# Attention sums divided untransposed, eight heads at a time, and the rows of maxima loaded from ScalarE's queue

## What is computed

```python
def _L0_xattn_ref(x, cross_input, ...):        # H, D = 16, 16
    q, k, v = _heads(x @ Wq + bq), _heads(x @ Wk + bk), _heads(x @ Wv + bv)
    att = einsum('bhqd,bhkd->bhqk', q, k) * scale, causal mask
    y = einsum('bhqk,bhkd->bhqd', softmax(att), v)
    qc, kc, vc = ...                            # the same against cross_input, 1601 keys, no mask
    y = y + einsum('bhqk,bhkd->bhqd', softmax(attc), vc)
    return y.transpose(0, 2, 1, 3).reshape(B, T, C) @ Wp + bp

x = x + tanh(g_xattn[0]) * _L0_xattn_ref(_layernorm(x), ctx_512, ...)
x = x + tanh(g_ffn[0]) * _L0_ffn_ref(_layernorm(x), ...)   # shared expert + 2 of 7 routed experts, 704 wide
```

## Time and profile before

| | |
|---|---|
| median of three runs | 1414.64 us (1413.62 to 1415.73) |
| the profiled execution | 1413.27 us |
| its span, first to last instruction | 1411.5 us |
| PE busy | 1368.6 us (97%) |
| DVE, ACT, POOL busy | 880.9, 727.3, 365.4 us |
| granted TensorE clock, mean | 0.993 |

### The profile page before, as it was taken

How to read it: one execution, slowest core, us unless ns; L and a number is a source line. 1 busy time by engine, 2 the same in 40 slices (tenths; PEclk the granted TensorE clock), 3 DMA queues, 4 the chain that set the end, 5 groups by cost and what they waited for, 6 DMA issues and landing times.

```text
span 1411.5 us, 27301 instructions
## 1 busy us (share of the span) xinstructions
PE 1368.6 (97%) x7688; PEld 694.0 (49%) x7689; DVE 880.9 (62%) x1804; ACT 727.3 (52%) x1107; POOL 365.4 (26%) x743
## 2 busy tenths in 40 slices
PE   7988999999999999999999999989999999999997
PEld 4544333333333333333333333364556777777775
DVE  6776888888888888888888888653532222222221
ACT  4644667677777676767676767732210222222221
POOL 5655222222222222222222222200001232233232
PEclk9999999999999999999999999999999999999999
DMA  8754111111111111111111111057004122112111
GB/s 246 237 186 154 43 53 51 48 50 48 47 49 50 51 50 50 49 48 48 48 51 51 50 49 50 7 218 297 0 1 134 26 33 34 30 30 37 30 30 23
DMA packets 57711, 98.43 MB, mean 70 GB/s; under 512 B 7441, under 2 KB 42001, under 8 KB 56657
## 3 DMA queue, kind: packets, MB, share of 16 engines
q1 hardware_dynamic: 50384, 88.10, 18.8%
q0 software_dynamic: 7296, 9.97, 4.5%
HBM read 69.20 MB, written 28.58 MB: 69 GB/s over the span
## 4 chain that ended last, share of the span: by engine, by line
PE 88%; DMA 2%; DVE 2%; ACT 1%; issue 1%; POOL 1%; SPq 0%; POOLq 0%; ACTq 0%; DVEq 0%
PE ps L669 19%; PE ps L834 13%; PE ps L651 13%; PE ps L551 13%; PE ps L847 7%; PE ps L786 5%; PE ps L797 3%; PE ps L718 3%; PE ps L654 2%; PE ps L565 2%; PE ps L858 2%; DMA k_parts<-work 2%; PE ps L555 1%; PE ps L592 1%; PE ps L625 1%
## 5 line engine op out<-in xcount | busy, mean ns | idle before, releaser
L1242 DVE TENSOR_REDUCE mx<-ps 128x1 f32<-128x512 f32 (+1 forms) x832 | 515.1, 662 | 99.6 <-PE ps L551 69.3
L993 ACT ACTIVATE arena<-ps 128x1024 f32<-128x1024 f32 (+1 forms) x512 | 484.3, 995 | 138.7 <-PE ps L651 135.2
L669 PE MATMUL ps<-arena 128*32 128x512 f32 (+5 forms) x2432 | 290.9, 525 | 0.6 <-ACT arena L993 0.4
L551 PE MATMUL ps<-arena 96*128 96x512 bf16 x768 | 263.0, 382 | 7.3 <-DMA arena<-k_parts 2.9
L651 PE MATMUL ps<-arena 98*128 98x512 bf16 x832 | 264.4, 381 | 5.0 <-DMA arena<-rowst 4.9
L1144 POOL TENSOR_SCALAR_AFFINE_SELECT arena<-arena 128x128 f32<-128x128 f32 x256 | 74.8, 292 | 439.2 <-ACT arena L993 429.3
L834 PE MATMUL ps<-arena,work 128*128 x608 | 186.4, 460 | 0.6 <-issue 0.6
L551 PEld LDWEIGHTS ps<-arena 96*128 96x128 bf16 x768 | 74.1, 96 | 178.0 <-DVE mx L1242 103.2
L1520 DVE TENSOR_TENSOR work<-work,ps 128x352 f32<-128x352 f32 x76 | 39.6, 521 | 179.1 <-ACT work L1061 179.1
L834 PEld LDWEIGHTS ps<-arena,work 128*128 128x128 f32 x608 | 112.5, 190 | 57.4 <-issue 1.1
L1242 DVE TENSOR_REDUCE mneg<-ps 128x2 f32<-128x512 f32 (+2 forms) x192 | 112.4, 640 | 23.9 <-PE ps L561 23.4
(11 more groups left out here) (161 smaller groups left out, 1406.8 us busy)
## 6 DMA issues: line engine op xcount, KB each, us to landing
arena<-in_experts SPq DMA_DIRECT2D x8, 2176.0 KB, 12.2
arena<-k_parts SPq DMA_DIRECT2D x64, 198.1 KB
arena<-k_parts SPq DMA_DIRECT2D x64, 132.1 KB
arena<-q_parts SPq DMA_DIRECT2D x64, 96.0 KB
k_parts<-work SPq DMA_DIRECT2D x16, 300.0 KB, 5.2
q_parts<-work SPq DMA_DIRECT2D x12, 384.0 KB, 5.4
arena<-k_parts SPq DMA_DIRECT2D x64, 66.0 KB
arena<-q_parts SPq DMA_DIRECT2D x64, 64.0 KB
```

The source lines that it names most:

```text
L551: mm = pe.matmul(out, qx[:, qt * P:(qt + 1) * P], ks[0:KROWS, T + j * CHUNK:T + (j + 1) * CHUNK], start=True, stop=True)
L669: mm = pe.matmul(ps[32 * q:32 * q + VW, 6, b0:b1], vst[0:kn, r % VR, TT + kt if cross else kt, :], pr[0:kn, c0:c0 + b1 - b0], start=(phase ...
L993: act.activation(pr[:, c0:c0 + n], ps[:, 2 * (g % 2):2 * (g % 2) + 2, :].rearrange("p b n -> p (b n)")[:, 0:n], ACT.Exp, scale=SCALE).then ...
L1242: return dve.tensor_reduce(m, out, AX_X, ALU.max)
```

## The change

- The `norm` step is gone from PE, and with it `norm_out`, POOL's operations per head and the reciprocal per head. Its place among the banks stays, as `spare`. Whoever would have waited for `norm` now waits for the entry six places before.
- `osb` of each head is stored to DRAM (`o_parts`, 256 KB) by SP. ACT's next copy into `osb` waits for the store.
- Eight heads are a group. Their denominators come back as 128 x 32 for each of four parts, their numerators as 128 x 512 (16 rows a head), the first part straight into `yT`, the channel-by-token layout that `project` reads. POOL adds the cross parts, DVE takes one reciprocal of 128 x 64, SP stores it and loads it back spread over each head's 16 rows. POOL multiplies twice and adds once.
- The steps are now 4 alone, seven turns of eight heads, 4 alone. The group's loads are issued in the turn's fourth head, the sums are made in its sixth, the reciprocal in its seventh, the products in its eighth.
- `rows` on ACT issues the load of `rowst` itself, behind its own copy.
- The fourth stack slot lies in `shared`. The shared expert's weights are loaded behind the store of head 60.
- At the end there is no turning of y. Sequences 0 to 2 are projected, then `turn_xn(0)` and one piece of `shared_up(0)`, then sequence 3. The last head's parts of the last group are copied out of `osb` by SP (denominators) and ACT (numerators). ACT also issues the first store of `xn_rows`.

```diff
@@ schedule
-            out += [("values", 0), ("norm",)]
+            out += [("values", 0), ("spare",)]
@@
+SUMS_IN, RECIP_IN, OUT_IN, RECIP_AT = 5, 6, 7, 3
 def run_steps(eng, step):
-    step(0, 0, False, True, True)
-    step(1, 1, True, True, True)
-    heads = NR
-    turns = (NU - 2 - 2) // heads
...
+    for u in range(BEGUN):
+        step(u, u % NR, u > 0, True, True)
+    with eng.Fori(0, TURNS) as i:
+        for h in range(GH):
+            step(i * GH + (BEGUN + h), h % NR, True, True, True, i, h)
+    for u in range(GH * TURNS + BEGUN, NU):
+        step(u, u % NR, True, u + 1 < NU, u + 2 < NU)
@@ sync
-            rows_load(0, 0)
...
+            def sums_store(v):
+                sp.wait_ge(S["o_evac"], v + 1)
+                sp.dma_start(o_parts[bass.ds(v, 1)].rearrange("a p t -> (a p) t"), osb).then_inc(S["o_written"], 16)
+            def parts_load(j, n=GH):
+                sp.wait_ge(S["parts_free"], j + 1)
+                sp.wait_ge(S["o_written"], j * (16 * GH) + 16 * n)
+                heads = o_parts[bass.ds(j * GH, n)]
+                for q in range(4):
+                    src = heads[:, VW * q + D:VW * q + D + 1, :].rearrange("u a (d t) -> (u a) d t", t=DW)
+                    sp.dma_start(den[0:n * D, q, :], src).then_inc(S["den_in"], 16)
+                for q, dst in enumerate([yT[:, bass.ds(j, 1), :].rearrange("p a t -> p (a t)"), *cross_num, self_num]):
+                    sp.dma_start(dst[0:n * D, :], heads[:, VW * q:VW * q + D, :]).then_inc(S["num_in"], 16)
+            def recip_store(j):
+                sp.wait_ge(S["recip_done"], j + 1)
+                for s in range(2):
+                    sp.dma_start(recip_rows[...], recip[:, s, :]).then_inc(S["recip_out"], 16)
+            def recip_load(j):
+                sp.wait_ge(S["recip_out"], j * 32 + 32)
+                for s, dst in enumerate((cross_recip, self_recip)):
+                    sp.dma_start(dst, src.to_broadcast([GH, D, T])).then_inc(S["recip_in"], 16)
...
+                    stack_loads(i * GH + (BEGUN + NR + h), h % NR)
+                    sums_store(i * GH + (BEGUN + h))
+                    if BEGUN + h == GH - 1:
+                        parts_load(i)
+                    if h + 1 == RECIP_IN:
+                        recip_store(i)
+                        recip_load(i)
+            for u in range(TURNS * GH + BEGUN, NU - 1):
+                sums_store(u)
+                if u == TURNS * GH + BEGUN:
+                    sp.dma_start(weights[:, SHARED, :], a["experts"][SHARED]).then_inc(S["shared_load"], 16)
+            parts_load(NGRP - 1, GH - 1)
@@ tensor
-                    elif item[0] == "norm" and prev:
-                        bank_free(u, "norm")
-                        norm(u)
...
-            for b in range(B):
-                if b == B - 1:
-                    turn_xn(0)
+            for b in range(B - 1):
                 project(b)
+            turn_xn(0)
             pe.wait_ge(S["shared_load"], 16)
-            shared_up(0)
+            shared_up(0, 0, SPLIT_UP)
+            project(B - 1)
+            shared_up(0, SPLIT_UP, IT)
@@ scalar
                 act.activation(rowst[:, :], out[0:MROWS * 2 * TT, 0:P], ACT.Copy).then_inc(S["rows_evac"], 1)
+                act.wait_ge(S["rows_evac"], v + 1)
+                act.dma_start(qst[r][KROWS:KROWS + MROWS, :, :].rearrange("p i t -> p (i t)"), rowst[:, :]
+                              ).then_inc(S["rows_ready"], 16)
...
+                if not (isinstance(u, int) and u == 1):
+                    act.wait_ge(S["o_written"], u * 16 - 16)
                 act.activation(osb[:, :], ps[:, 6, :], ACT.Copy).then_inc(S["o_evac"], 1)
@@ gpsimd
+                pool.tensor_tensor(den[:, 0, :], den[:, 0, :], den[:, 1, :], ALU.add).then_inc(S["den_half"], 1)
+                pool.tensor_tensor(den[:, 2, :], den[:, 0, :], den[:, 2, :], ALU.add).then_inc(S["den_sum"], 1)
...
+                pool.tensor_tensor(y, y, cross_num[0], ALU.add).then_inc(S["num_half"], 1)
+                pool.tensor_tensor(y, y, cross_num[1], ALU.add).then_inc(S["num_sum"], 1)
...
+                pool.tensor_tensor(y, y, cross_recip, ALU.mult).then_inc(S["y_cross"], 1)
+                pool.tensor_tensor(self_num, self_num, self_recip, ALU.mult).then_inc(S["y_self"], 1)
+                pool.tensor_tensor(y, y, self_num, ALU.add).then_inc(S["y_done"], 1)
@@ vector
+            def reciprocals(j):
+                dve.wait_ge(S["den_sum"], j + 1)
+                dve.reciprocal(recip[:, :, :], den[:, 2:4, :]).then_inc(S["recip_done"], 1)
...
+            for t in range(early):
+                residual(t)
...
+                if t == 4:
+                    reciprocals(NGRP - 1)
+            tail_stats(early - 1)
+            for t in range(early - SCALE_LAG, early):
+                tail_scale(t)
+            shared_hidden(0, 0, SPLIT_UP)
+            for t in range(early, NT):
+                residual(t)
```

More of the change, by code:

```diff
@@ L117 @@
 PE_ORDER = schedule()
-ENTRIES = [item for item in PE_ORDER if item[0] in ("max", "norm", "rows")]
+ENTRIES = [item for item in PE_ORDER if item[0] in ("max", "spare", "rows")]
 RING = 3
@@ L124 @@
 SCALE_LAG = 5
-RSUM_AT = HALF + 4
-def run_steps(eng, step):
-    step(0, 0, False, True, True)
-    step(1, 1, True, True, True)
-    heads = NR
-    turns = (NU - 2 - 2) // heads
[L134 to L137, removed]
+SPLIT_UP = 1
+GH = P // D
+NGRP = NU // GH
+BEGUN = GH // 2
+TURNS = NGRP - 1
+SUMS_IN, RECIP_IN, OUT_IN, RECIP_AT = 5, 6, 7, 3
+assert GH % NR == 0 and BEGUN % NR == 0 and BEGUN >= 2
+def run_steps(eng, step):
+    for u in range(BEGUN):
[4 more added lines that the diff above has]
+    for u in range(GH * TURNS + BEGUN, NU):
         step(u, u % NR, True, u + 1 < NU, u + 2 < NU)
@@ L577, in bank_free @@
                         pe.wait_ge(S["max_red"], min(n, NU * NMAX - MAXED) if isinstance(n, int) else n)
-                elif before[0] == "norm" and not (isinstance(u, int) and u == 0):
-                    pe.wait_ge(S["norm_evac"], step)
                 elif before[0] == "rows":
@@ L709, in step @@
                     pe.wait_ge(S["pool_chain"], 3 * NR + 3)
-            def norm(u):
-                if isinstance(u, int) and u > 1:
-                    pe.wait_ge(S["norm_evac"], u - 1)
-                pe.wait_ge(S["o_evac"], u)
-                out = bank_of("norm")
-                for t in range(TT):
-                    mm = pe.transpose(out[:, t * P:(t + 1) * P], osb[:, t * P:(t + 1) * P], ident[:, :])
-                mm.then_inc(S["norm_mm"], 1)
             pe.wait_ge(S["prep_freed"], len(pieces))
@@ L973, in sums_out, with step @@
                 act.wait_ge(S["pv_done"], u * NPH)
+                if not (isinstance(u, int) and u == 1):
+                    act.wait_ge(S["o_written"], u * 16 - 16)
                 act.activation(osb[:, :], ps[:, 6, :], ACT.Copy).then_inc(S["o_evac"], 1)
[L976 to L984 removed]
+            def step(u, r, prev, nxt, nxt2, group=None, h=None):
                 for g in range(NG):
@@ L1155, in step @@
                 mask(u, 1, 2)
-                if prev:
-                    cross_sums(u)
                 mask(u, 2, TT)
-                if prev:
-                    head_output(u)
-                    pool.wait_ge(S["y_done"], u)
+                if h == SUMS_IN:
+                    den_sums(group)
+                    num_sums(group)
+                if h == OUT_IN:
+                    outputs(group)
             pool.wait_ge(S["prep_freed"], len(pieces))
@@ L1378, in tail_scale, with residual @@
                 scale_rows(t)
-            for t in range(NT):
+            def residual(t):
                 dve.wait_ge(S["proj_mm"], t + 1)
```

202 lines of the change are left out of this document (105 added, 97 removed).

## The result

The changed kernel takes 1471.45 us (median of four runs, 1465.92 to 1474.85) where the kernel before took 1414.13 in the same comparison: 1.040 times as long, 95% interval 1.0364 to 1.0435. The forecast was 1386.1 us, with a range of 1374 to 1404.

A forecast was written before the change was run, and what follows sets the result against it. PE looked like the only bound, but after the norm the loop hangs on DVE. Gains of 4.5 (start), 17.5 (loop), 1.0 (last heads) and 5.5 (tail), 28.5 in all, gave 1384.8 profiled, 1386.1 us as median; range 1374 to 1404.

The forecast's parts named there:

- the loop's side work: Loop: added ACT issue, POOL operations, DVE reciprocal and SP transfers (8.4 us of issue once in eight heads) cost nothing.
- 1.8 to 3.4: Loop, SP: expected landing time in us of a transfer, from two earlier loads, on an idle queue and behind stores.
- 3.2 was the limit: Loop, score matmul: the rows' load delays PE only if it lands later than 3.2 us after issue.
- Rival 4: Score matmul in every head: rows land late, each of 61 heads loses 0.6 us, 1423 us; chance 0.06.
- rival 3: Loop: POOL's 128x512 operations reach masks or small DVE operations, 21 us lost, 1407; sign: longer heads, one kind in eight; 0.07.
- The gain in the loop: Steps 1 to 61: without the norm DVE's reductions start earlier, 0.287 us a head, 17.5 us in all.
- the last heads: Steps 62 and 63: no pair pieces there, so the norm's 0.50 us goes whole, 1.0 us in all.
- rival 1: Loop: PE alone counts, 0.50 us gained in each of 61 steps, 30.5 us, time 1373; chance 0.14.
- rival 2: Loop: the stall moves and the loop gains nothing; start, last heads and tail remain, 1403.6 us; chance 0.16.
- The start: Before the loop: rows from ACT's queue land earlier, first exp at 136.0; 4.5 us gained (3 to 7).
- The tail: After the last values: norm chain and y turns go, third shared product 5.5 us sooner (2 to 9.2).
- the delay costs nothing: Tail, SP queue: expert loads start some 12 us later, harmless because 70 us without a load follow.

The follow-up runs named there:

- run 3: Changed kernel with every stack load cut into 16-row ones, twelve issues a head instead of six: 1395.31 us, 0.9883 times the kernel before.
- run 8: Changed kernel with only the keys' stack loads cut into 16-row ones: 1410.59 us, 0.9999 times the kernel before.
- run 9: Changed kernel with only the queries' stack loads cut into 16-row ones: 1437.65 us, 1.0174 times the kernel before.
- Run 1: Changed kernel with the load of the maxima's rows issued by SP again, behind the stack loads and the sums' store: 1511.19 us.
- run 6: Changed kernel with all stack loads cut into 16-row ones and expert loads issued only after the first store of normalised rows landed: 1382.45 us, 0.978.
- run 7: Changed kernel with the group's eight loads and the reciprocals' store and load moved into the next head, behind its stack loads: 1474.28 us, 1.0416.
- run 11: run 6 with the group's eight loads and the reciprocals' store and load one head later, as in run 7: 1442.89 us, 1.0218.
- run 4: Kernel before the change with only the load of the rows issued from ACT's queue: 1410.2 us, 0.9978.
- run 5: Kernel before the change with only its 48- and 32-row stack loads cut into 16-row ones: 1406.05 us, 0.9941.
- run 12: Changed kernel, stack loads uncut, with only the expert loads waiting for the first store of normalised rows: 1457.89 us, 1.0318.
- run 10: run 6 with the last group's and last head's denominator loads issued ahead of that group's numerator loads: 1385.91 us, 0.9819.

## Why the prediction was wrong

**The step that failed** is the loop's side work: "SP: per head one store of 256 KB, once in eight heads eight loads and four small transfers ... So nothing". I priced SP's issue time and asked whether the stack loads would be late for PE. They weren't. I didn't ask what the new transfers meet in the DMA engines. They had room as an average, a share of 0.14, but two of them were busy for most of a head. The store landed in 7.4 us where I had "1.8 to 3.4", and SP stands for it; then group loads, stack loads and rows arrive together, and PE goes on 6.58 us after the rows' issue where 3.2 was the limit. Two of the "four small transfers" weren't small either: the reciprocals' loads write 256 KB each. Price: 77 us over the clean pace (815.5 against 62 x 11.93 = 739.7 less 1.1 for the last, shorter one). PE's wait for the rows is 42.0 of it; by the two windows above most of the rest is matmuls at the lower clock behind PE's stops.

What shows this is the share of 0.12 with the stack loads alone in flight, and the row of runs 3, 8 and 9. The Trainium skill, in the section named at runs 8 and 9, says how the number comes about: a transfer takes the largest count up to 16 that divides the slowest dimension (other than 1) of both sides, and from SP and ACT always the lowest-numbered engines. Here the slowest dimension of the source is 3 or 2 parts, and with one part alone its 16 rows. The trace agrees with the counts; it has no number of the engine for a packet, so that these are the lowest ones is not shown here. For the group's loads the slowest dimension of the source is the 8 heads, and the trace has eight packets in flight (share 0.50). A form of these loads that uses all sixteen was not tried. The Trainium skill's section "Issuing engines are not separate DMA queues" of the same page, cited in the forecast, says that transfers run on the same 16 engines whoever issues them. Run 1 and the changed kernel agree: ACT's queue shielded the rows from SP's waits, not from its bytes.

**Rival 4** was the way it went in kind ("the load from ACT's queue shares the engines with SP's stores and stacks", slower), at 0.06. I had every head late by 0.6 us; it was two in eight, by 2.5 to 6.7. My argument against it, "at that point of the head SP has nothing to issue in seven of eight heads", held in six, and left out that an exception could cost ten times the 0.6. A condition that fails rarely has to be priced where it fails. The sign that I had named for rival 3, longer heads of one kind in eight, would have misled: the longer heads came, and PE waited in them for the rows, the sign of rival 4.

**The gain in the loop** was right. "A period of 12.0 us where it was 12.3": 11.93 in ordinary heads; DVE's idle behind the small operations gone; L645 still waits for DVE. An ordinary head gained 0.35 us (12.28 to 11.93) where the sum had 0.287. Run 6 shows the loop without most of the damage: 744.7 us for 62 heads against 760.5, 15.8 gained of 18.5 forecast for the loop and the last heads; eight heads are still 12.4 to 13.8 us there. Rivals 1 (0.50 a head) and 2 (nothing) are out by that. **Rival 3**, POOL meeting the masks, was not seen in the changed kernel; runs 7 and 11 show that it comes at once when the loads for POOL are later.

**The start**: 4.2 gained of 4.5. PE's first scores came at 133.76 (forecast 133), the first exp at 136.59 (136.0). Head 1's rows were on the chain for 3.36 us from their issue at 144.86, but PE had other work and stood only about 0.1 us. In run 6 the matmul for head 1 comes at 133.62, 14.4 us earlier than before, where runs 4 and 5 alone gave 6.4 and 3.2. That the changed kernel gained 4.2, so near the forecast, while the cut of the stack loads brings it 10 more, makes the hit here partly luck. Which part of the 14.4 belongs to what, I didn't try.

**The tail**: forecast 5.5 gained, 9.4 lost up to the third shared product. "The expert loads ... the delay costs nothing" looked at whether the weights come in time. It didn't ask what stood behind them: the delay puts them just ahead of ACT's store of 512 KB, for which the silu waits. Runs 6 and 12 show it from both sides, 12.9 and 13.6 us. With the wait the stretch is 29.3 us, 3.3 gained of 5.5. The denominators landed 4.7 us after issue, later than the forecast had it, which would be about the size of the missing 2.2. But run 10 brought that landing forward and the stretch grew, so the cause of the 2.2 is not shown.

Both misses are one mistake: each new or moved transfer was checked for the one who needs it, and not for those that stand behind it. With the two mended, run 6 is at 1382.45 us where the forecast, made without them, had 1386.1; the sum's terms differ (the start more, loop and tail less), so this is partly luck.

## What to carry to other kernels

For every transfer that an edit adds or moves, work out the bytes on the busiest DMA engine, not the mean over sixteen, and name what is queued behind it there. A DMA share that stays near a small multiple of 1/16 while large loads are in flight is the sign of loads that use few engines (0.12 and 0.50 here). A small load on the critical path that lands at once in the old profile has shown its luck, not its margin; look how long before its first packet the engines ran dry (0.04 us here, 604.66 to 604.70).

## What the runs showed of the hardware

- A 256 KB store took 7.4 us as a median beside loads on two and three engines, 2.1 us beside the same bytes spread, and 3.1 and 6.1 between.
- Six more issues in each head on SP (12 instead of 6) cost nothing that shows: the period stayed 11.93 us.
- A 512 KB store issued 2.1 us behind the first of two 2176 KB loads from another queue took 16.1 us; with the loads behind it, 4.4 in the same kernel (run 12) and 3.8 in run 6.
- In run 6 a scaling of a tile by DVE (128x256) took 1.44 us at 902.58, beside a POOL sum of 1.26 us (128x512) from 902.61; its neighbours took 0.39. In the changed kernel there were two such cases, 1.44 us at 984.26 and 1.13 at 992.48. In the forecast 1 us stood for it, so the size was about right.
- The rows' load of 4 KB had its first packet 1.3 us after the issue in each head of the kernel before from head 2 on, and 3.9 to 5.0 us in the 14 long heads of the changed one.
- What stays open: of the 6.58 us of the load at 252.40, 4.38 passed before its first packet, 1.55 from there to its last, and 0.65 until PE could go on. The packet records have no engine, and so don't tell whether the load stood in the engines behind packets of SP's queue or got its own packets late.
